# One store of the row maxima instead of two, the softmax inverses one head earlier, and split loads of the modulation rows

## What is computed

```
mod = (silu(c) @ wmod) -> sa, ca, ga, sb, cb, gb          # rows 0..5 of each batch
h = layernorm(x) * (1 + ca) + sa
Q = h @ Wq.T (16 heads of 16);  K, V from 64 latents
logits = causal(q_lat @ latent_k.T / 8);  attn = softmax(logits);  x = x + ga * (heads @ Wout.T)
h = layernorm(x) * (1 + cb) + sb
scores = sigmoid(h @ gate.T); each of 16 experts takes its best 512 tokens
x = x + gb * (sum of experts' silu(g) * up @ down, plus a shared silu feed-forward)
```

## Time and profile before

| | us |
|---|---|
| median of 3 runs | 1226.83 |
| the profiled execution, its own time | 1228.18 |
| its span, first to last instruction | 1226.5 |
| TensorE busy (matmul) | 1120.3 |
| VectorE busy | 858.3 |
| ScalarE busy | 600.0 |
| GpSimd busy | 642.5 |
| mean granted TensorE clock | 0.958 |

### The profile page before, as it was taken

The page is one execution under the profiler, slowest core; times in us unless marked ns, Lnnn a source line. Parts: engine busy times, 40 slices in busy tenths (PEclk is TensorE's granted clock), DMA queues, the critical chain, the costliest instruction groups (busy, mean ns, idle before and its releaser), DMA issues.

```text
span 1226.5 us, 21562 instructions
## 1 busy us (share of the span) xinstructions
PE 1120.3 (91%) x7422; PEld 875.4 (71%) x7422; DVE 858.3 (70%) x2174; ACT 600.0 (49%) x1085; POOL 642.5 (52%) x680
## 2 busy tenths in 40 slices
PE   4988988998898889999788999999999999999997
PEld 3545655555555457888677888888888888888886
DVE  5677797797786536778866776677776677776662
ACT  2247777776775563322143554444554444554441
POOL 4124476575573655222326666656666656666654
PEclk9679999999998789999999999999999999999998
DMA  5836768868778435875544445554545554556531
GB/s 168 104 51 112 110 123 169 168 134 173 142 141 161 140 104 181 205 202 145 159 127 116 144 123 159 126 133 116 145 124 158 126 130 119 145 122 160 126 87 18
DMA packets 100588, 165.46 MB, mean 135 GB/s; under 512 B 18680, under 2 KB 65272, under 8 KB 98432
## 3 DMA queue, kind: packets, MB, share of 16 engines
q1 hardware_dynamic: 84096, 137.86, 45.7%
q0 software_dynamic: 14336, 25.70, 10.9%
q10 hardware_dynamic: 2048, 0.53, 0.3%
HBM read 103.97 MB, written 34.13 MB: 113 GB/s over the span
## 4 chain that ended last, share of the span: by engine, by line
PE 34%; POOL 24%; issue 18%; DVE 9%; DMA 8%; SPq 3%; ACT 3%; ACTq 1%; POOLq 0%; DVEq 0%
POOL HTl L1642 12%; PE LB L761 6%; PE MB L761 6%; PE LB L505 4%; POOL out_y L1690 4%; PE MB L505 4%; POOL XG L1649 4%; DMA HT<-Us 3%; PE UB L505 3%; PE LB L598 3%; DVE junk L1167 3%; PE UB L614 2%; PE XB L505 2%; SPq L304 2%; DMA XT<-hD 2%
## 5 line engine op out<-in xcount | busy, mean ns | idle before, releaser
L1642 POOL TENSOR_TENSOR HTl<-HF,HTh 128x512 fp32r<-128x512 f32 x160 | 222.9, 1398 | 242.9 <-ACT HTh L973 242.7
L1167 DVE CUSTOM_DVE_ANT_0 junk<-MB,MK 128x256 bf16<-128x256 f32 (+3 forms) x512 | 219.8, 484 | 63.8 <-PE MB L575 62.4
L1553 POOL TENSOR_SCALAR_AFFINE_SELECT P<-P 128x256 f32<-128x256 f32 x256 | 101.4, 420 | 143.0 <-ACT P L913 143.0
L598 PE MATMUL LB<-QS,KS 50*128 50x256 f32 (+3 forms) x512 | 129.4, 372 | 16.2 <-ACT P L911 13.5
L973 ACT ACTIVATE HTh<-HF 128x512 fp32r<-128x512 f32 x160 | 100.4, 627 | 89.4 <-DVE HF L1429 89.4
L1690 POOL DMA_INDIRECT out_y<-EO,IDX x64 | 106.6, 1666 | 69.2 <-DVE EO L1516 63.7
L575 PE MATMUL MB<-KS,QS 48*128 48x256 f32 (+3 forms) x512 | 134.2, 377 | 8.0 <-DVE NM L1167 4.6
L911 ACT ACTIVATE P<-LB 128x768 f32<-128x768 f32 x128 | 103.8, 811 | 75.6 <-PE LB L598 75.1
L980 ACT ACTIVATE SIL<-LB,gbT 128x512 f32<-128x512 f32 x64 | 43.8, 685 | 185.4 <-PE LB L505 181.2
L598 PEld LDWEIGHTS LB<-QS,KS 50*128 50x128 f32 x512 | 83.2, 201 | 64.6 <-issue 46.5
L761 PE MATMUL LB<-WDh,HTh 128*128 128x256 f32 x320 | 94.3, 295 | 18.0 <-POOL HTl L1642 17.9
(11 more groups left out here) (265 smaller groups left out, 3011.1 us busy)
## 6 DMA issues: line engine op xcount, KB each, us to landing
WR<-in_gw SPq DMA_DIRECT2D x16, 1024.0 KB
WR<-in_uw SPq DMA_DIRECT2D x16, 1024.0 KB
WR<-in_dw SPq DMA_DIRECT2D x16, 1024.0 KB
QS<-ST SPq DMA_DIRECT2D x96, 128.0 KB, 4.8
KS<-ST SPq DMA_DIRECT2D x96, 128.0 KB, 5.9
hD<-h SPq DMA_DIRECT2D x8, 1024.0 KB, 5.5
XT<-hD SPq DMA_DIRECT2D x8, 1024.0 KB, 10.3
X<-in_x SPq DMA_DIRECT2D x8, 512.0 KB, 6.5
```

Of the source, the lines that this page charges most:

```text
L598: m = e.matmul(LB[:, o:o + w], KS[base:base + 50, k, j * 128:(j + 1) * 128], QS[base:base + 50, k, 128 * j:512], start=True, stop=True)
L1167: m = e.tensor_tensor_reduce(junk[:, o:o + w], MB[:, o:o + w], MK[:, 512 - w:512], 1.0, -3e38, ALU.add, ALU.max, NM[:, k // 4, 4 * (k % 4) ...
L1553: m = e.affine_select(out=dd, in_=dd, compare_op=ALU.is_ge, fill=0.0, base=0, pattern=[[0, 2], [1, 128]], channel_multiplier=-1)
L1642: e.tensor_tensor(HTl[:, slot, :], HF[i][:], HTh[:, slot, :].bitcast(F32), ALU.subtract).then_inc(g_ht, 1)
```

## The change

It has five parts. (1) VectorE copies the 16 finished columns of NM twice beside each other into a new tile NM2 (128 x 32). TensorE transposes that, so that ScalarE's NMh and NMf have 32 rows, twice the same 16. One operation with a factor PC (0 in rows 0 to 15, -1 in rows 16 to 31) makes NMx: the rounded value in the first 16 rows, the difference in the others. (2) ScalarE's queue stores NMx with one DMA to rows 48 and 49 of QS, instead of two. (3) The reciprocal is issued after head 3 instead of head 4 on VectorE, its store on SP at `k = 4` instead of 5 and ahead of `stack(u+2, 0)`, and the read back at `k = 5` instead of 6 and ahead of `take_heads(u, 0)`. (4) `load_bt` fetches its three rows with three DMAs (1 KB pieces) instead of one (3 KB pieces), in another order of rows. (5) The constants get 4 columns more, and PC is loaded from them by a DMA of its own at the start; the first transposes wait for both.

```
@@ sync_program
         def load_bt(b):
-            e.dma_start(BT[b % 2][:].rearrange("p i d -> p (i d)"),
-                        modD[b:b + 1, 2:5, :].rearrange("b r d -> b (r d)").broadcast_to([128, 3 * D])).then_inc(c_bt[b % 2], 16)
+            for i, r in enumerate((2, 4, 3)):
+                e.dma_start(BT[b % 2][:, i, :], modD[b, r:r + 1, :].broadcast_to([128, D])).then_inc(c_bt[b % 2], 16)
...
-        e.dma_start(C[:], cst).then_inc(c_cst, 16)
+        e.dma_start(C[:], cst[:, 0:512]).then_inc(c_cst, 16)
+        e.dma_start(PC[:], cst[:, 512:516]).then_inc(c_cst, 16)
...
-                if k == 5 and u:
+                if k == 4 and u:
                     inverses(u - 1)
                 if k == 4 and u + 2 < NU:
                     stack(u + 2, 0)
-                if k == 6 and u:
+                if k == 5 and u:
                     spread_inverses(u - 1)
                 if k == 5:
                     take_heads(u, 0)
@@ tensor_program
         def put_max(u, half):
-            e.wait_ge(d_mx, 3 * n_head(u, 4 * half + 3) + 3 + (1 if u + 1 < NU or half == 0 else 0))
-            e.transpose(MB[0:16, 1280:1408], NM[:, half, :], ident).then_inc(p_mt, 1)
+            e.wait_ge(d_nm2, 2 * u + half + 1)
+            if u + 1 < NU or half == 0:
+                e.wait_ge(d_mx, 3 * (n_head(u + 1, 0) if half else n_head(u, 4)) + 1)
+            e.transpose(MB[0:32, 1280:1408], NM2[:, half, :], ident).then_inc(p_mt, 1)
@@ scalar_program
-                e.wait_ge(c_nm[half], 32 * u)
-            e.activation(NMh[half][:], MB[0:16, 1280:1408], ACT.Copy, scale=-1.0)
-            e.activation(NMf[half][:], MB[0:16, 1280:1408], ACT.Copy, scale=-1.0).then_inc(a_nm, 1)
+            e.activation(NMh[half][:], MB[0:32, 1280:1408], ACT.Copy, scale=-1.0)
+            e.activation(NMf[half][:], MB[0:32, 1280:1408], ACT.Copy, scale=-1.0).then_inc(a_nm, 1)
...
-            for r, part in enumerate((NMh, NMl)):
-                e.dma_start(QS[base + 48 + r:base + 49 + r, 4 * half:4 * half + 4, :].rearrange(
-                    "p h (i t) -> p (h i) t", t=128).bitcast(F32), part[half][:].bitcast(F32)).then_inc(c_nm[half], 16)
+            e.dma_start(QS[base + 48:base + 50, 4 * half:4 * half + 4, :].rearrange(
+                "p h (i t) -> p (h i) t", t=128).bitcast(F32), NMx[half][:].bitcast(F32)).then_inc(c_nm[half], 16)
@@ vector_program
+            if k % 4 == 3:
+                e.wait_ge(d_mx, 3 * n + 3)
+                if 2 * u + k // 4 >= 2:
+                    e.wait_ge(p_mt, 2 * u + k // 4 - 1)
+                e.tensor_copy(NM2[:, k // 4, :].rearrange("p (r q) -> p r q", r=2),
+                              NM[:, k // 4:k // 4 + 1, :].broadcast_to([128, 2, 16])).then_inc(d_nm2, 1)
...
-            e.tensor_tensor(NMl[half][:], NMf[half][:], NMh[half][:].bitcast(F32), ALU.subtract).then_inc(d_nm, 1)
+            e.scalar_tensor_tensor(out=NMx[half][:], in0=NMh[half][:].bitcast(F32), scalar=PC[0:32, 0:1],
+                                   in1=NMf[half][:], op0=ALU.mult, op1=ALU.add).then_inc(d_nm, 1)
...
-                if k == 4 and u:
+                if k == 3 and u:
                     inverses(u - 1)
```

More of the change, by code:

```diff
@@ L113, in block_program @@
     halfc = at("halfc", 89216, [128, 4])
+    PC = at("PC", 225568, [128, 4])
     st2, mv2 = at("st2", 89248, [128, 4, 6]), at("mv2", 89344, [128, 4, 2])
@@ L130, in block_program @@
     NM = at("NM", 186016, [128, 2, 16])
-    NMf = [at(f"NMf{i}", 225600 + 512 * i, [16, 128]) for i in range(2)]
-    NMh = [at(f"NMh{i}", 186144 + 512 * i, [16, 128], F32R) for i in range(2)]
-    NMl = [at(f"NMl{i}", 187168 + 512 * i, [16, 128], F32R) for i in range(2)]
+    NM2 = at("NM2", 225600, [128, 2, 32])
+    NMf = [at(f"NMf{i}", 225856 + 512 * i, [32, 128]) for i in range(2)]
+    NMh = [at(f"NMh{i}", 186144 + 512 * i, [32, 128], F32R) for i in range(2)]
+    NMx = [at(f"NMx{i}", 187168 + 512 * i, [32, 128], F32R) for i in range(2)]
     junk = at("junk", 188192, [128, 1280], BF16)
@@ L218, in block_program @@
     d_own = sem("d_own")
+    d_nm2 = sem("d_nm2")
     d_hf, d_cut, d_tb, d_eo, d_top, d_oh, d_idx, d_xt = (sem(n) for n in (
@@ L590, in main @@
             if k % 4 == 0:
-                e.wait_ge(c_nm[k // 4], 32 * (u + 1))
+                e.wait_ge(c_nm[k // 4], 16 * (u + 1))
             for j in (2, 1, 3, 0):
@@ L635, in tensor_program @@
         m.then_inc(p_fold, 1)
-        e.wait_ge(c_cst, 16)
+        e.wait_ge(c_cst, 32)
         hT(0, 0, "p0")
@@ L1163, in maxima @@
                 if u and k % 4 == 0:
-                    e.wait_ge(p_mt, 2 * (u - 1) + k // 4 + 1)
+                    e.wait_ge(d_nm2, 2 * (u - 1) + k // 4 + 1)
                 for i in blocks:
@@ L1173, in put_max @@
             if u:
-                e.wait_ge(c_nm[half], 32 * u)
-            e.tensor_tensor(NMl[half][:], NMf[half][:], NMh[half][:].bitcast(F32), ALU.subtract).then_inc(d_nm, 1)
+                e.wait_ge(c_nm[half], 16 * u)
+            elif half == 0:
+                e.wait_ge(c_cst, 32)
+            e.scalar_tensor_tensor(out=NMx[half][:], in0=NMh[half][:].bitcast(F32), scalar=PC[0:32, 0:1],
+                                   in1=NMf[half][:], op0=ALU.mult, op1=ALU.add).then_inc(d_nm, 1)
         def inverses(u):
@@ L1183, in outproj @@
             e.wait_ge(p_out, 2 * b + i + 1)
-            e.wait_ge(c_bt[b % 2], 16 * (b // 2 + 1))
+            e.wait_ge(c_bt[b % 2], 48 * (b // 2 + 1))
             if 2 * b + i:
@@ L1451, in vector_program @@
                 e.wait_ge(c_tab, 16 * (NB - 1))
-                kept(e.tensor_tensor(th[:, 0:2, :], th[:, 0:2, :], BT[1][:, 2:3, :].broadcast_to([128, 2, D]), ALU.mult))
+                kept(e.tensor_tensor(th[:, 0:2, :], th[:, 0:2, :], BT[1][:, 1:2, :].broadcast_to([128, 2, D]), ALU.mult))
                 settled()
-                e.tensor_tensor(H2[:, 0:2, :], th[:, 0:2, :], BT[1][:, 1:2, :].broadcast_to([128, 2, D]),
+                e.tensor_tensor(H2[:, 0:2, :], th[:, 0:2, :], BT[1][:, 2:3, :].broadcast_to([128, 2, D]),
                                 ALU.add).then_inc(g_h2, 1)
@@ L1579, in shift2 @@
                 e.wait_ge(c_tab, 16 * b)
-            e.wait_ge(c_bt[b % 2], 16 * (b // 2 + 1))
-            kept(e.tensor_tensor(th[:, ks, :], th[:, ks, :], BT[b % 2][:, 2:3, :].broadcast_to([128, 2, D]), ALU.mult))
+            e.wait_ge(c_bt[b % 2], 48 * (b // 2 + 1))
+            kept(e.tensor_tensor(th[:, ks, :], th[:, ks, :], BT[b % 2][:, 1:2, :].broadcast_to([128, 2, D]), ALU.mult))
             settled()
-            e.tensor_tensor(H2[:, ks, :], th[:, ks, :], BT[b % 2][:, 1:2, :].broadcast_to([128, 2, D]), ALU.add).then_inc(g_h2, 1)
+            e.tensor_tensor(H2[:, ks, :], th[:, ks, :], BT[b % 2][:, 2:3, :].broadcast_to([128, 2, D]), ALU.add).then_inc(g_h2, 1)
         kept(e.memset(halfc[:], -0.5))
@@ L1705, in constants @@
     p = np.arange(128)
-    cst = np.zeros((128, 512), np.float32)
+    cst = np.zeros((128, 516), np.float32)
     cst[:, 0:128] = np.eye(128)
@@ L1710, in constants @@
     cst[:, 384:512] = p[None, :]
+    cst[16:32, 512] = -1.0
     cpos = np.zeros((128, 512 * 3), np.float32)
```

## The result

The changed kernel takes 1234.08 us (median of 8 runs, 1232.12 to 1238.22), the kernel before beside it 1226.8 us (8 runs). The ratio is 1.0056, with a 95% interval of 1.003 to 1.0084: slower, where the forecast was 1220.8 us, faster. Only the range, 1211 to 1235, held it. The profiled execution took 1237.99 us, with a span of 1236.3.

What follows compares the result with a forecast made beforehand. Before 450 us, few waits that empty VectorE and TensorE were taken to bound the kernel, notably SP held by rdD. Terms -5.3 + 5.2 - 2.7 - 1.3 - 1.5 = -5.6, say -6 us, gave 1220.8 us; range 1211 to 1235.

Steps and rivals of the forecast that it cites:

- The reciprocal and its two DMAs one head earlier: Attention: HT lands 3.0 us earlier, VectorE is through 1.05 us sooner in each of 5 pairs of units; -5.3 us.
- the first rival: Attention: HT lands when it did and VectorE stands longer before the reciprocal; +10 us, 1236.5 us, chance 0.15.
- can only make HT earlier: SP, odd units: the next stack, issued behind the waiting reciprocal, could only speed HT, by nothing to about 3 us more.
- The copy: VectorE's copies to NM2 with their wait, and the even unit's reciprocal ahead of ST: 0.75 us in 7 pairs, +5.2 us.
- One store: ScalarE's queue: 32 fewer DMAs and an earlier store of the maxima; -2.7, -1.3 and -1.5 us.
- The second rival: Single store of the maxima, dealt by its 2 rows over two DMA engines, lands 2.1 us later; 1237.8 us, chance 0.1.
- a landing well over 5.1 us with TensorE waiting for it: Sign that the forecast is wrong: NMx, the stored maxima, lands well over 5.1 us after issue and TensorE waits.
- BT in three DMAs: SP, ahead of D and HT: two more issues of 0.5 us, hidden because they end before Us is ready; nothing.
- PC: Start of the kernel: its load lands 0.6 us behind C while the chain is in VectorE's weights; nothing.

Runs made afterwards that it cites:

- e3: The kernel before with only the reciprocal and its two DMAs one head earlier; 1237.41 us, ratio 1.0065 to the kernel before.
- e7: The kernel before with the reciprocal and its two DMAs one head earlier, but SP issuing the stack ahead of rdD at head 4; 1240.84 us, ratio 1.0132.
- e11: The kernel before, with SP in odd units issuing the first stack of the unit after next behind rdD; 1249.12 us, ratio 1.012.
- e14: The changed kernel with the store to tab and the loads of BT two steps later in odd units, behind D and HT; 1223.27 us, ratio 0.994.
- e15: The kernel before with only the store to tab and the load of BT two steps later in odd units; 1223.81 us, ratio 0.9941.
- e4: The kernel before with the copy to NM2, NMx and the load of PC, but still two stores; 1235.07 us, ratio 1.0034.
- e2: The kernel before with the copy to NM2, NMx, the load of PC and the single store; 1229.49 us, ratio 1.0007.
- e1: The changed kernel with rows 48 and 49 of QS stored by two DMAs again; 1242.63 us, ratio 1.0093 to the kernel before.
- e5: The kernel before with the reciprocal and its two DMAs one head earlier in even units alone; 1232.65 us, ratio 1.006.
- e8: The kernel before with only BT loaded by three DMAs; 1227.57 us, ratio 0.9994.
- e6: The kernel before with the reciprocal one head earlier on VectorE alone, SP's list unchanged; 1250.21 us, ratio 1.0203.
- e12: The kernel of e2 with VectorE's reciprocal one step later in odd units, SP's order as in the kernel before; 1223.57 us, ratio 0.9957.

## Why the prediction was wrong

**The failed step is the first, "The reciprocal and its two DMAs one head earlier", taken at -5.3 us; alone it measures +8 us (e3).** Its own figures came out close. I shifted HT's landing by 3.0 us; counted from unit 7's first maxima difference the reciprocal's start is at +15.71 before and +13.02 after, 2.7 earlier. I had VectorE stand 4.4 us in unit 7; it stood 4.34. I had it through 1.05 us sooner: reciprocal and difference are done at +15.62 (244.76 + 0.60) instead of +16.06, 0.44 sooner. What failed is the inference from VectorE's gain to the kernel's:

- The step counted SP's earlier issues as gain only. DN leaves 5.0 us sooner relative to the work, the stack 3.5 and tab 3.7, and the store of the maxima on ScalarE's queue, whose place is fixed by the work, is now behind tab and BT. It lands 8.9 us after its issue in the four odd units of the table, where it was 6.7, and TensorE's wait for it went from 2.7 to 20.7 us (60 to 450 us). I had written that "the DMA engines are full" for the first rival, and asked it of HT alone.
- VectorE's stop moved ahead of a head's maxima. I named TensorE's transposition as queued behind and gave it no price: its wait went from 2.2 to 8.0 us with part 3 alone (e3), and to 12.4 in the whole change, of which the copy has a part. The step also counted only what VectorE does there, not what VectorE waits for. Before, the row at that place is

```profile
236.91 0.42 DVE L1167 CUSTOM_DVE_ANT_0 junk<-MB,MK 128x256 bf16<-128x256 f32 x1 [2.81 <-PE MB L575]
```

  and now the logits are there after the stop (243.03, no wait), but the next head's are not (247.13, 1.17 us). From the end of head 3 to head 5's first maximum it was 234.10 to 242.36, 8.3 us; now, from the copy's start, 238.10 to 247.13, 9.0, of which 0.3 is the copy. In this unit the loop through TensorE took back about what VectorE had gained.
- That holding the stack behind rdD "can only make HT earlier" was right (e3 against e7, e11). But it has a price, TensorE's wait for KS in e11, which I didn't look for.

**The first rival** ("HT lands when it did, and VectorE stands longer", 1236.5 us) had about the right time by luck: HT did land earlier in the pair, which it denies. What it says for itself, that the DMA engines and not the issue set the landing, is what e14 and e15 show to matter.

**The copy** was taken at +5.2 us. It takes 0.27 us and NMx 0.05 more than NMl (0.340 against 0.294); e4 gives +4.2 (0 to 8.4), which fits.

**One store** was taken at -5.5 us; e4 to e2 gives -0.27% (-3.3 us), e1 to after -0.37% (-4.5). That fits in sign and is a little large, though neither is clear of nothing. The second rival, built on the dealing of a store by its rows, has the dealing right by the packets (1088) and the price wrong: in e2 the store lands no later, and the time is the same. Its sign, a landing well over 5.1 us with TensorE waiting for it, came all the same, and e5 and e1 show it with two stores too; it marks what lies ahead of the store. Whether the single store adds something of its own there (8.9 us on average after, 6.9 in e1, 8.4 in e5) stays open. The Trainium skill ("DMA: Bandwidth & Descriptors", section "Why a DMA increments its semaphore by 16 and not by 1") has a DMA run on the largest number of engines up to 16 that divides the slowest dimension of both its sides, which is 2 here; the packets of q10 agree with that.

**BT in three DMAs** at nothing: e8, 0.9994. Right: the three issues end at 230.73 + 2.26 = 232.99, and Us, which D waits for, is written at 232.94, so they are just hidden. (My sum took 0.7 us for tab's issue, where the earlier trace rows has 1.72; 229.1 instead of 228.1 would still have been under 229.5.) **PC** at nothing: e4 and e2 hold it, no cost seen.

With the parts other than the first at about nothing together (e2, 1.0007), the whole is the first step. What its price should have been could not be had by adding waits. TensorE's two waits grew by 28.2 us together, but its wait for ScalarE's exponents fell from 13.5 to 5.8 us in the same stretch, and all its idle time in attention grew by 8.3.

## What to carry to other kernels

Here an engine that issues DMAs and was held back by a wait also spaced its traffic; when such a wait goes, ask which small, urgent transfer of another queue has so far been leaving ahead of the bulk and is now behind it. Put bulk that nobody wants soon (here tab and BT, 896 KB) behind the small ones that somebody waits for: that one move was worth 0.6% with no other change, though the waits explain only a part of it. A long wait is not a gain in waiting: GpSimd's 28.5 us for DN stand in the fastest kernel of all, and the change that took most of them away was slower.

## What the runs showed that I had not expected

- A DMA's landing hung on what another queue of the core had issued just before. The store of the maxima landed 7.7 to 9.4 us after its issue right behind tab and BT, and 5.8 to 7.6 at the same places ahead of them; the median of all the 8 KB stores before was 5.1.
- One DMA over two rows left 1088 packets where two DMAs had left 2048, as if cut over two engines, and with nothing else changed at this place (e2) the store of 16 KB landed no later for it.
- How much order alone is worth: tab and BT two heads later in SP's list gave -0.6% (e15), VectorE's reciprocal one head earlier +2.0% (e6), one head later in odd units -0.5% (e12 against e2), all with the same work.
